# A block of attention and experts on one core: row statistics of two tiles by one instruction, shorter tile sums, and five changes of order

## The reference, cut to what matters

```python
# x: 32 sequences of 256 rows of 128; all float32
h = _layernorm(x, axis=-1) * (1 + ca) + sa
x = x + ga * attn(h)                      # below
h = _layernorm(x, axis=-1) * (1 + cb) + sb
x = x + gb * experts(h)                   # 8 experts, one for each row: argmax of h @ centroids.T

# attn: cumulative sums along the 256 rows of a sequence
K = exp(h Wk1' + bk1);  S = cumsum(K * h) / (cumsum(K) + 1e-6);  O_ar = S * sigmoid(h Wq1' + bq1)
E = h - O_ar shifted by a row;  S2 = cumsum(sigmoid(k * (h Wk2' + bk2) shifted) * E)
out = (O_ar + S2 * Q2) Wproj' + bproj

# experts: of the rows of expert e
y = relu((layernorm(h) * ln_g + ln_b) W1 + b1) W2 + b2;  out = h + y
```

## Time and profile before

| | |
|---|---|
| median of 3 runs | 335.1 us (332.93 to 335.32) |
| the profiled execution | 336.69 us, its span 335.0 us |
| mean granted TensorE clock | 0.964 |
| busy: PE, DVE, ACT, POOL | 297.9, 268.0, 248.6, 237.4 us |
| attention phase / expert phase | about 0 to 165 us / 175 us to the end |

### The profile page before, as it was taken

How to read it: one execution, slowest core, us unless ns; L and a number is a source line. 1 busy time by engine, 2 the same in 40 slices (tenths; PEclk the granted TensorE clock), 3 DMA queues, 4 the chain that set the end, 5 groups by cost and what they waited for, 6 DMA issues and landing times.

```text
span 335.0 us, 8136 instructions
## 1 busy us (share of the span) xinstructions
PE 297.9 (89%) x1889; PEld 237.1 (71%) x1889; DVE 268.0 (80%) x926; ACT 248.6 (74%) x556; POOL 237.4 (71%) x370
## 2 busy tenths in 40 slices
PE   8797998898989989899898999999999999888930
PEld 7474555564656656465587899999999999888930
DVE  5798999999999999989886387898666665758850
ACT  2759788989899999999768666776677776766510
POOL 7984334787989888978646878778888855544770
PEclk9979779999999999999799999999999999999985
DMA  7343288424438786634396789877888777778300
GB/s 213 80 117 94 80 241 217 127 63 155 157 116 233 208 233 200 168 103 149 104 291 206 229 269 302 284 238 228 229 226 234 208 238 226 220 232 233 102 18 0
DMA packets 49429, 60.87 MB, mean 182 GB/s; under 512 B 5557, under 2 KB 38095, under 8 KB 49379
## 3 DMA queue, kind: packets, MB, share of 16 engines
q1 hardware_dynamic: 42806, 43.11, 47.0%
q0 software_dynamic: 6368, 16.82, 13.7%
q10 hardware_dynamic: 208, 0.41, 0.3%
HBM read 39.90 MB, written 20.87 MB: 181 GB/s over the span
## 4 chain that ended last, share of the span: by engine, by line
PE 53%; DVE 13%; issue 13%; ACT 11%; POOL 3%; SPq 2%; DMA 1%; POOLq 0%; ACTq 0%; DVEq 0%
PE bank L845 15%; PE bank L817 13%; PE bank L639 3%; PE bank L821 3%; PE bank L742 2%; POOL out_dram L613 2%; PE bank L745 2%; PE bank L783 2%; DVE shared L1234 2%; PE bank L735 2%; PE bank L691 2%; PE bank L830 2%; PE bank L766 2%; ACT shared L947 2%; PE bank L714 1%
## 5 line engine op out<-in xcount | busy, mean ns | idle before, releaser
L613 POOL DMA_INDIRECT out_dram<-shared,ids x71 | 72.1, 1015 | 34.2 <-DVE shared L1709 15.9
L538 POOL DMA_INDIRECT expert_rows<-rows,slots x64 | 65.5, 1023 | 15.8 <-issue 15.4
L845 PE MATMUL bank<-w_all,shared 128*128 x568 | 69.4, 275 | 0.4 <-issue 0.3
L845 PEld LDWEIGHTS bank<-w_all,shared 128*128 128x128 f32 x568 | 66.2, 192 | 0.9 <-issue 0.9
L1044 ACT ACTIVATE shared<-bank,par 128x256 f32<-128x256 f32 x100 | 40.9, 472 | 15.3 <-PE bank L817 15.3
L501 POOL TENSOR_SCALAR zz<-rows,negm,rstd 128x128 f32<-128x128 f32 x64 | 33.4, 532 | 24.8 <-ACT rstd L1025 17.3
L817 PE MATMUL bank<-shared,early 128*128 128x256 f32 x200 | 47.8, 382 | 0.3 <-ACT shared L1044 0.3
L817 PEld LDWEIGHTS bank<-shared,early 128*128 128x128 f32 x200 | 36.1, 190 | 4.5 <-issue 0.3
L493 POOL TENSOR_SCALAR xh<-x_in,negm,rstd 128x128 f32<-128x128 f32 x64 | 28.6, 458 | 9.0 <-DVE shared L1207 8.6
L1501 DVE TENSOR_TENSOR shared<-bank,b_bc 128x256 f32<-128x256 f32 (+1 forms) x42 | 14.7, 366 | 23.6 <-PE bank L845 22.9
L1064 ACT ACTIVATE shared<-bank,par 128x256 f32<-128x256 f32 (+1 forms) x46 | 22.7, 515 | 6.4 <-PE bank L830 4.0
(11 more groups left out here) (216 smaller groups left out, 699.6 us busy)
## 6 DMA issues: line engine op xcount, KB each, us to landing
early<-in_L_ffn_W_dram SPq DMA_DIRECT2D x25, 256.0 KB
x_in<-expert_rows SPq DMA_DIRECT2D x15, 385.0 KB, 4.2
rows<-in_L_ffn_W_dram SPq DMA_DIRECT2D x21, 256.0 KB
x_in<-in_L_attn_x_dram SPq DMA_DIRECT2D x16, 256.0 KB, 3.2
rows<-gates_rows SPq DMA_DIRECT2D x32, 128.0 KB, 5.2
full<-expert_rows SPq DMA_DIRECT2D x10, 385.0 KB
expert_rows<-pad_rows SPq DMA_DIRECT2D x9, 385.0 KB, 8.4
full<-expert_rows SPq DMA_DIRECT2D x11, 192.5 KB
```

Of the source, the lines that this page charges most:

```text
L538: pool.indirect_dma_start(rows_dram, bass.IndirectOffsetOnAxis(ap=slots[:, c * CN + t:c * CN + t + 1], axis=0), rows[:, c % RR, t, :], Non ...
L613: pool.indirect_dma_start(out_rows, bass.IndirectOffsetOnAxis(ap=ids[:, u % IR, t:t + 1], axis=0), u_sb[:, k, t, :], None, bounds_check=T - 1,
L845: mm = pe.matmul(out_at(o, t), hid[:, k, f, t * P:(t + 1) * P], of_expert(w2_all, e, f * D, (f + 1) * D), start=(f == 0), stop=(f == FC - 1))
```

## The change

1. One `bn_stats` takes two tiles: their elements are read in turns, so that the even ones are the first tile's and the odd ones the second's. Its six results are count, mean and squared deviation of both tiles, and `bn_aggr` is left out everywhere. The division by 128 goes into ACT's Ln (`scale=1/D`) or POOL's first instruction. ACT still negates the means.
2. `ranks(g)` adds a tile's counts only up to the first tile of the next group. The next group begins with one product that spreads that tile's slots, which DVE copied out (`carry`), over its own tiles.
3. POOL multiplies the gated weights right behind normalising x, in place of after normalising z and the scatters.
4. PE makes the logits and turns h back before it multiplies Oar.
5. POOL takes a tile's row numbers after the stores of the same turn, three turns later than before.
6. Around the last steps: a z pair behind `error_sum` in step 14, eight filler transposes before the last queries, expert numbers read earlier by ACT, and the statistics of z (`rstd_of(NC - 2)`) ahead of `sum_of(NC - 1)`.

```diff
@@
-            pool.iota(base_i[:, :, :], pattern=[[0, NT], [RS, E]], base=FT, channel_multiplier=0).then_inc(s_iota, 1)
+            pool.memset(base_bf[:, GT + 1:, :], 0.0).then_inc(s_const, 1)
+            pool.iota(base_i[:, :, :], pattern=[[0, GT + 1], [RS, E]], base=FT, channel_multiplier=0).then_inc(s_iota, 1)
...
-                pool.tensor_scalar(veps[:, a, :], mv[:, a, 0, :, 1], LN_EPS, None, ALU.add).then_inc(s_vx, 1)
+                pool.wait_ge(s_bnx, CN // 2 * (a + 1))
+                pool.tensor_scalar(veps[:, a, :], bn[:, a, 0, :, 2], 1.0 / D, LN_EPS, ALU.mult, ALU.add).then_inc(s_vx, 1)
...
@@
                     normalise_x(a)
+                if 0 <= c < 6:
+
+                    pool.wait_ge(s_E, c + 1)
+                    for m in ((2, 3), (4, 5), (6, 7, 8), (9, 10, 11), (12, 13), (14, 15))[c]:
+                        gate_weights(m)
...
-                if 0 <= c < 6:
-
-                    pool.wait_ge(s_E, c + 1)
-                    for m in ((2, 3), (4, 5), (6, 7, 8), (9, 10, 11), (12, 13), (14, 15))[c]:
-                        gate_weights(m)
...
@@
-            for j in range(-3, NJ + 2):
-                if in_b(j + 3):
-                    take_ids(j + 3)
+            for j in range(NJ + 2):
                 if j in (2, 3):
...
                             store(stored)
                             stored += 1
+                if in_b(j):
+
+                    take_ids(j)
...
@@
+                last = min((g + 1) * GT, NT - 1)
+                if g > 0:
+                    pe.wait_ge(s_dconst, 13)
+                    pe.wait_ge(s_base, g)
+                    pe.matmul(ps_rank[:, (g * GT + 1) * E:(last + 1) * E].rearrange("p (t e) -> p t e", e=E),
+                              seq_mask[0:1, 1:P + 1], carry[0:1, g:g + 1, :].to_broadcast([1, last - g * GT, E]),
+                              start=False, stop=True, skip_group_check=True)
...
-                    if first < NT:
-                        mm = pe.matmul(ps_rank[:, first * E:].rearrange("p (t e) -> p t e", e=E), ones_bf[:, :],
-                                       oh[:, t:t + 1, :].to_broadcast([P, NT - first, E]), start=False, stop=True, skip_group_check=True)
+                    if first <= last:
+                        mm = pe.matmul(ps_rank[:, first * E:(last + 1) * E].rearrange("p (t e) -> p t e", e=E),
+                                       ones_bf[:, :], oh[:, t:t + 1, :].to_broadcast([P, last + 1 - first, E]), start=False, stop=True, skip_group_check=True)
...
@@
+                if in_a(z):
+                    logits(z)
+                    turn_back(z)
+                if in_a(c):
                     pe.wait_ge(s_Oar, c + 1)
                     pe.wait_ge(s_wg, c + 1)
...
-                if in_a(z):
-                    logits(z)
-                    turn_back(z)
                 if in_a(n):
                     keys(n)
                 if c == -2:
                     queries(0)
+                if c == NC - 2:
+
+                    keep_going(8, ps_t)
...
@@
-                act.activation(lnv[:, i, 1, :], mv[:, i, 1, :, 1], ACT.Ln, bias=epsv[:, :]).then_inc(s_lnv, 1)
+                act.activation(lnv[:, i, 1, :], bn[:, i, 1, :, 2], ACT.Ln, scale=1.0 / D, bias=epsv[:, :]).then_inc(s_lnv, 1)
...
+                if c == NC - 1:
+
+                    act.wait_ge(s_planned, 1)
+                    of_first = [expert_of(act, n) for n in range(2)]
                 if in_a(z):
                     rows_of(z)
...
             act.wait_ge(s_par, 1)
-            act.wait_ge(s_planned, 1)
             rstd_of_tile(0)
             turned_z(NC - 3)
             rstd_of_tile(1)
             experts = [norm_of_expert(0)]
+            rstd_of(NC - 2)
             sum_of(NC - 1)
-            rstd_of(NC - 2)
...
@@
+            def stats_of_two(into, rows_of_two):
+
+                return dve.bn_stats(into.rearrange("p t k -> p (t k)"), rows_of_two.rearrange("p t d -> p d t"))
...
+                stats_of_two(bn[:, a, 0, 2 * h:2 * h + 2, :], x_in[:, a % XR, 2 * h:2 * h + 2, :]).then_inc(s_bnx, 1)
...
+                stats_of_two(bn[:, o + 6, 1, 2 * h:2 * h + 2, :], rows[:, o % RR, 2 * h:2 * h + 2, W:W + D]
+                             ).then_inc(s_bnz, 1)
...
+                    if g + 1 < NG:
+
+                        dve.tensor_copy(carry[0:1, g + 1, :], ps_rank[0:1, (g + 1) * GT * E:((g + 1) * GT + 1) * E]
+                                        ).then_inc(s_base, 1)
...
@@
-                if in_a(o):
+                if in_a(o) and not first:
                     z_stats(o, 0)
-                    z_stats(o, 1)
...
+                if first:
+                    z_stats(o, 0)
                 if in_a(o):
-                    z_stats(o, 2)
-                    z_stats(o, 3)
+                    z_stats(o, 1)
```

## The result

The changed kernel takes 331.5 us (median of 9 runs, 329.77 to 331.94), the kernel before 333.0 us in the same comparison (9 runs, 332.19 to 335.32). The ratio is 0.9918, with a 95% interval of 0.9889 to 0.9948: about 2.7 us, or 0.8%, faster. (The two medians alone differ by 1.5 us, the two means by 2.5.) Medians here are over all executions of a kernel, while the ratios leave out disturbed ones, which took longer, such as one of stats_only that took 513.48 us at a mean granted clock of 0.555. I had forecast 329.3 us and 1.8%. The sign, the range and the main mechanism held; the size did not. The profiled execution of the changed kernel has a span of 330.1 us (331.93 us of its own time), against 335.0 (336.69) before, so the two traces differ by 4.9 us, which is more than the kernels do; the profiled execution of before is longer than all nine of that comparison.

What follows compares the result with a forecast made beforehand. DVE was taken to bound the attention phase narrowly, with ACT, PE and POOL close behind. Terms 2.6 + 0.45 + 2.15 + 0.9 + 0.1 - 0.2 = 6.0 us, 336.7 to 330.7, scaled to the median and called 329.3; range 326 to 335.

Steps and rivals of the forecast that it cites:

- Statistics: DVE in the attention phase: 0.9 us off each step, ten steps shrink to the ACT and PE floor, 2.6 us gained.
- (1): DVE's interleaved statistics read is slow, 0.60 us each; 334.2 us, no difference that counts; chance 0.20.
- (2): DVE's interleaved read takes over twice the time per element, making the kernel slower, up to 348.6 us; chance 0.08.
- rival (3): POOL or h2T raises the step floor to 9.55, or fillers don't hold the clock; 330.8 us; 0.24 together with (4).
- Start: The fourth x block on DVE, before the first cumulative sum, ends earlier: 0.45 us gained, nothing if the read is slow.
- Early steps: Attention steps before 50 us wait on PE and ACT, not DVE, and stay as they are: no gain.
- Short sums: PE's sums within a group: 0.4 us in group 0, inside the 2.6; extra product costs 0.2 in the expert phase.
- Last steps: Step 14: fillers hold the clock, 1.75 us, and the z pair leaves PE's wait for the sum, 0.4 us.
- Logits first: PE makes logits ahead of Oar products: h2T cover fits by 0.1 us, worth nothing; if it fails, PE stalls.
- Change of phase: ACT's waits before the first two experts' scales go, with expert numbers read earlier: 0.9 us gained (0.3 to 1.4).
- Tail: End of kernel: number-taking between POOL's stores costs 0.2 us, DVE's statistics return 0.3, together 0.1 gained.
- rival (4): Expert phase starts sooner, but last tiles wait for SP's loads and POOL's stores; about 331 us; 0.24 together with (3).

Runs made afterwards that it cites:

- stats_only: The kernel before with the two-tile statistics alone, every other order kept; ratio to the kernel before 0.9881 (0.9846 to 0.9917).
- means_early: The changed kernel with ACT's negated means moved ahead of h2T; ten attention steps took 93.81 us in place of 94.63.
- contig_x: The changed kernel with x statistics read in memory order (x means and variances then wrong); 411 ns an instruction, 417 interleaved.
- ranks_whole: The changed kernel with sums of slots over all tiles again, without the carried row; ten steps 95.29 us, ratio to the kernel before 0.982.
- before_again: The kernel before, without an edit, traced a second time; 334.1 us, a span of 331.5.
- logits_late: The changed kernel with logits and turn back of z behind the Oar products again; ratio to the kernel before 0.9856 (0.9766 to 0.9947).
- ids_first: The changed kernel with POOL taking row numbers three tiles ahead of the stores again; ratio to the kernel before 0.9897 (0.9838 to 0.9957).

## Why the forecast was right in sign and too large

**Statistics: right.** I took 0.33 us for an instruction; it takes 0.34. Ten steps were to shrink by 2.6 to a floor of 9.40 that ACT and PE share, and shrank by 2.3 to 2.5 to 9.42. means_early, where a shorter path on ACT alone shortens the step, shows that ACT is in that floor. Rivals (1) and (2), the slow interleaved read, are out by contig_x, and of rival (3) the higher floor of POOL or h2T.

**Start: right.** From the first turn of x to the first cumulative sum it takes 3.20 us (8.44 to 11.64) for 3.61 (10.19 to 13.80): 0.41 for 0.45. Over all traces it is 3.54 and 3.61 before, and 3.01 to 3.22 with the new statistics. The other 1.75 us between the two traces at this point is the start of the executions.

**Early steps: a term that I put at nothing.** I wrote that the steps before 50 us wait on PE and ACT, not DVE, and stay. For one of them this is wrong: from the fifth turn to the sixth at full clock it takes 8.17 or 8.18 us for 9.13, and the wait of 0.72 us for DVE's sum that stood in it is gone. That is 0.95 us, though from a single trace of before at full clock there.

**Short sums: right in the steps, not priced apart.** The 0.4 that I counted inside the 2.6 is 0.66 by ranks_whole: 0.30 in the step of group 0 and 0.33 in a later one, where I had expected nothing. In the expert phase relu to SP's tail takes 88.0 us (mean of three) for 87.8 (mean of two), 0.25 more, for the +0.2 that I took. With a spread of 0.8 in those three it is an agreement, not a proof.

**Last steps: the step that failed.** I had "1.75 + 0.4 us" there. The 1.75 was the half clock of one execution, read as a property of the kernel; before_again has the same wait and no fall. That is the term that was mis-sized, with 0 in its place. It was also read too large for that execution: I compared the 4.44 us of the three groups with the 2.68 of another step, but at this place and full clock they take 2.90 (160.02 to 162.92 in before_again), so the fall cost 1.54. As rival (3) had it, the fillers don't hold the clock over these steps: seven of the ten traces that have them show a fall there. The 0.4 fell too. The queries start 0.34 us earlier, 15.13 us after the sixteenth turn for 15.47. But the z pair that I moved off PE's wait for the sum now stands in its wait for the Mp pass: in before_again 1.58 us from the sum to the Mp pass, in the changed kernel 1.86, and PE waits twice, 0.37 and 0.20 us. From the queries to the turn of z it takes 3.88 us for 3.47, and the 0.34 is gone. From the first query to the Mp products it is 2.29 for 2.01, so 0.28 of the 0.41 is this wait; the rest is in the Mp products and the sums of slots with their carried row. No run moves the z pair back by itself.

**Logits first: the step whose condition I named and did not follow into the last step.** I wrote that it costs nothing "but if the cover fails, PE stalls with the Oar products ... behind it". The cover was counted in a middle step alone. In the last one ACT has a table load and three small operations ahead of h2T, PE waits 1.19 us, and 0.85 is lost (logits_late). A wait of 0.95 to 1.19 us there was also followed by the lower clock within the next 6 us (0.72 on the mean of these) in four of the eight traces that have it (ids_first, means_early, ranks_whole, contig_x), and in none of the six without it. But in five of those six the clock falls in the last steps too, only earlier. So it isn't shown that this wait costs a fall.

**Change of phase: right in kind, larger.** First scale 0.56 us behind the turn of the tile, for 1.37 and 1.78 in the two traces of before, and from the first scale to the first relu 2.44 for 3.01: 1.4 to 1.8 us for my 0.9. It pays for what the logits and the z pair lose: from the sixteenth turn to the relu 29.28 us for the 30.36 of before_again, 1.1 gained in all.

**Tail: wrong sign.** I had 0.1 gained. The stores first cost 0.59 (I had 0.2 for one number-taking; from 310 us on, three stand among the nine stores), and about 0.15 more lies between SP's last load and the last store. SP's tail itself took 41.1 (mean of three) for 40.4; these 0.7 us are single slow issues of SP in two of the traces (2.36 and 2.70 us for a pair of loads that mostly takes 1.44), and before_again has one of 2.17. Their cause, and that they belong to the change, is not shown. This was rival (4), in part: some of the gain ends in the tail.

The sum with the measured terms, against before_again where a fall of the clock would disturb: 0.4 + 2.4 + 1.1 - 0.25 - 0.65 - 0.75 = 2.25 us, beside 2.7 by the ratio, whose interval is 1.7 to 3.7. With the 0.95 of the early step, seen in one trace of before, it is 3.2. Either lies inside the interval, which is too wide to tell between them. Of the 3.75 us between 2.25 and my 6.0, 1.75 is the clock, 1.5 the tail (0.1 forecast, -1.4 measured), 0.2 the steps, 0.2 the last steps and the change of phase together (1.3 forecast without the clock, 1.1 measured), and 0.1 the rest.

## What to carry to other kernels

A stretch at half clock in one trace is a reading of that execution until a second trace of the same kernel shows it again: price it at its odds, not in full. When an instruction is moved off one wait, look at the next wait of the same consumer, since the instruction may now stand ahead of what that wait is for. Check the cover of a reordering in the first and the last pass of a loop by themselves; the steady middle said "fits by 0.1", and the last pass lost 0.85 us.

## What the runs showed that I had not expected

The even and odd elements of one bn_stats over two interleaved tiles give each tile's mean and sum of squared deviations with no aggregate, in 417 ns for 256 elements per partition, against 411 in the order of memory. Before, two statistics of 277 ns and two aggregates of 157 did this.

The clock fell to the lower level in one execution and not in the other of the same program behind the same wait: 1.43 and 1.42 us ahead of the same queries, 0.51 against 1.00. From the first to the sixth turn of x falls like this one go with up to 3.4 us between kernels that don't differ there (36.72 with none, 40.09 with two).

On ACT the 8-element L1030 costs 0.20 us of the queue when another operation follows it (as L1028 in the changed kernel, 100.42 to 100.62) and 0.31 when a table load does.

On the two other chips the kernel before took 369.4 and 364.8 us (medians) for 333.5 on the first. In the traces of the changed kernels most of this lies between the first relu and SP's tail (109 to 116 us for 88), and the ten steps of the attention phase agreed to 0.1 us. Why, no run shows.
